# Similarities from tokens times a weight product made on the chip, in place of queries times keys

## The chip, the cores and the metric

The kernel runs on one core of a Trainium2 chip. The metric is the device time of one execution in microseconds (us). TensorE is PE in the profile (PEld are its weight loads), VectorE is DVE, ScalarE is ACT, GpSimd is POOL, and SP issues the transfers.

## The reference

x has 4 batches of 256 tokens with 256 numbers; all is float32. Four layers follow each other, each on the layer norm of x and added to x:

1. an attention whose weights come from a context of 128 numbers a token;
2. a feed-forward layer (hidden size 1024, squared ReLU) whose two weight matrices are first quantised by blocks of 64, with a search over 16 scales;
3. a gated layer in which tokens and weights are scaled by column and by row and rounded to 8-bit integers ("the quantised layer");
4. a product-key expert layer, cut to its core:

```
q = (x @ Wq).reshape(b, t, H, 2, DK)              # H = 4, DK = 64
sim1 = einsum('bthd,hkd->bthk', q[..., 0, :], keys[:, :, 0, :])   # 128 keys
sim2 = einsum('bthd,hkd->bthk', q[..., 1, :], keys[:, :, 1, :])
s1, i1 = top_k(sim1, 8); s2, i2 = top_k(sim2, 8)
final_scores, pk_idx = top_k(s1[..., None] + s2[..., None, :], 8)  # of 64 pairs
hidden = silu(x . e_down[index]) * relu(final_scores)
out = sum over heads and chosen experts of hidden * e_up[index]    # 2048 experts
```

Nothing of x stands between Wq and the keys: a similarity is x times the product of a head's Wq columns (256 by 64) and its keys (64 by 128).

## The kernel before, in words

Each engine has one queue, and its order is written out by hand as a list of calls; engines wait for each other on counting semaphores. An engine does nothing past a call whose wait is not met. Tokens go in tiles of 128: batch b has tiles t = 2b and 2b + 1. PSUM is eight banks of 128 by 512 f32.

Up to some 147 us the attention and the search over scales run (calls `unit`, `square`, `sum_error`), interleaved. Then come, on PE:

- `ffn1(i)`, 16 groups of two matmuls with 512 columns (line 626), a ReLU on ACT (line 1169), a squaring on POOL (line 347); `ffn2(b, o, tiles)`, halves of the second product of batch b (line 772), into one bank a batch. When both halves of a batch are there, `x2(b)` on DVE adds them to X (line 1861) and takes the statistics of the norm.
- the quantised layer, per batch a long chain between the engines, all its PE steps in one bank (6, or 7 for batch 1): `c_x_transposed`, `c_ratio`, `c_root`, `c_factor`, `c_diag`, `c_factors` (line 789), `c_round` (lines 1891 to 1883), `c_integers`, `c_row_scales`, `c_clip`, `c_quantised_transposed`, `c_first`, `c_h`, `c_silu`, `c_a`, then the same steps again with a 2 in their names for the second product, `c_second`, and `x3(b)` on DVE. The buffers of the layer hold two batches.
- the expert layer: `pre(b)` transposes the normed tokens into bank 6, ACT copies them (`tokens_out`). `half_queries(b, lo, hi)` multiplies them by the query weights (line 869) into banks 4 and 5, and ACT copies the queries (`queries`, line 1436). `sims(b, n)` multiplies the queries of tile t by the keys (line 882): the two sides of a key lie on rows 0 to 63 and 64 to 127 of the array and go into banks 0 and 1, four heads of 128 columns each. DVE finds the 8 largest and their places (`top8`, lines 1976 and 1982), pairs them (`pair_top8`), looks up the expert numbers (`look_up`, lines 2002 to 2018) and builds masks (`mask`, `one_hots`, lines 2038 and 2042).
- `experts(b, lo, hi)` multiplies all 2048 rows of e_down by the tokens (line 898; 8 groups a batch, into banks 4 and 5 in turn), and ACT applies the silu (`gate`, line 1454). `scatter(b, n, half)` turns masks into coefficients (line 920), ACT copies these (line 1446), POOL or, for the last tiles, DVE multiplies them by the gates (`weigh`), and `up(b, n, lo, hi)` multiplies by e_up (line 934; 16 experts' rows at a time, 16 steps a tile). `result(t)` on DVE adds the tile to X (line 2066), and SP stores it.

An f32 matmul is two records on PE in the trace. The banks make the waits: banks 0 and 1 hold the similarities of one tile until `top8` of that tile has read them; banks 4 and 5 serve queries and experts in turn, so that

```
if b:
    pe.wait_ge(s["d_g_e"], 8 * b - 1 + i)     # queries: after gates of the batch before
...
if i < 2:
    pe.wait_ge(s["d_q_e"], 2 * b + 1 + i)     # experts: after the copies of the queries
```

The functions that the diff touches, with their callers:

## Time and profile before

| what | us |
|---|---|
| median of 3 runs | 388.55 (386.41 to 388.98) |
| the profiled execution, device time | 388.38 |
| its span, first to last instruction | 386.5 |
| busy in the span: PE, DVE | 340.7, 333.8 |
| busy in the span: ACT, POOL | 246.8, 140.2 |
| mean granted TensorE clock | 0.991 |

The span is one execution, and the 1.9 us between it and its device time lie around it. A granted clock of 1 is 2.4 GHz. Matmul records overlap, so a busy sum and a piece of the chain differ by some per cent.

### The profile page before, as it was taken

What the parts mean: (1) busy time and instruction counts of PE and PEld (TensorE: products, weight loads), DVE (VectorE), ACT (ScalarE), POOL (GpSimd) and SP (SyncE); (2) the same over time, 40 slices, a digit from 0 to 9 for tenths busy, and PEclk for the clock granted to TensorE, in tenths of its full rate; (3) what the DMA queues carried; (4) which work ended last, traced back from release to release, by engine and by line L of the source; (5) the groups of instructions that cost most, each with busy time, mean ns of one, the idle gap of its engine ahead of it and who ended that gap; (6) DMA issues with size and microseconds to landing.
All of it is one profiled execution on the core that took longest, in us unless ns stands there. A gap on an engine that the chain in (4) does not pass through costs nothing.

```text
span 386.5 us, 8279 instructions
## 1 busy us (share of the span) xinstructions
PE 340.7 (88%) x3222; PEld 249.5 (65%) x3222; DVE 333.8 (86%) x838; ACT 246.8 (64%) x371; POOL 140.2 (36%) x194
## 2 busy tenths in 40 slices
PE   2898796688889889999969889998999999989997
PEld 2455453243334337688948767887888887778886
DVE  3989999999989997368877999999999999999940
ACT  3899999999998992237456687755766654011000
POOL 8737524612665644211001104255424148601000
PEclk9999999999989999999998999999999999999999
DMA  8940000000000008000000000000000000000000
GB/s 252 358 137 3 1 0 0 2 0 2 2 0 0 2 1 270 2 0 3 0 2 0 3 0 3 0 3 2 2 17 16 2 15 4 2 15 2 17 15 27
DMA packets 11142, 11.40 MB, mean 29 GB/s; under 512 B 608, under 2 KB 10592, under 8 KB 11104
## 3 DMA queue, kind: packets, MB, share of 16 engines
q1 hardware_dynamic: 11104, 10.88, 8.7%
q8 instruction: 25, 0.41, 0.5%
q14 instruction: 13, 0.11, 0.1%
HBM read 9.83 MB, written 1.05 MB: 28 GB/s over the span
## 4 chain that ended last, share of the span: by engine, by line
DVE 46%; PE 31%; ACT 11%; issue 7%; DMA 2%; POOL 1%; SPq 1%; DVEq 0%; ACTq 0%; POOLq 0%
PE pair L934 7%; DVE arena L1663 6%; PE pair L772 5%; DVE arena L1653 4%; PE pair L626 3%; DVE i L1982 3%; DVE arena L2042 3%; PE pair L898 3%; DVE s L1976 3%; ACT arena L1200 2%; ACT arena L1203 2%; DVE arena L2038 2%; DVE XN L1588 2%; DMA arena<-in_L_ffn_keys_dram 2%; PE pair L920 2%
## 5 line engine op out<-in xcount | busy, mean ns | idle before, releaser
L1663 DVE TENSOR_REDUCE arena<-arena 128x16 f32<-128x1024 f32 x64 | 66.5, 1075 | 2.5 <-POOL arena L365 1.7
L898 PE MATMUL pair<-arena,EDT 128*128 128x256 f32 x256 | 60.2, 383 | 0.0
L934 PE MATMUL pair<-EU,arena 128*128 128x256 f32 x256 | 58.4, 382 | 0.6 <-DVE arena L2066 0.6
L934 PEld LDWEIGHTS pair<-EU,arena 128*128 128x128 f32 x256 | 47.9, 190 | 7.4 <-issue 1.0
L898 PEld LDWEIGHTS pair<-arena,EDT 128*128 128x128 f32 x256 | 47.1, 190 | 6.5 <-ACT arena L1454 0.2
L644 PE MATMUL pair<-arena,WQ 128*128 128x512 fp8e4 x112 | 33.8, 383 | 15.8 <-ACT arena L1203 7.8
L488 POOL TENSOR_TENSOR arena<-arena 128x512 f32<-128x512 f32 x20 | 27.6, 1394 | 45.1 <-ACT arena L1446 45.1
L1200 ACT ACTIVATE arena<-pair,sq_bias 128x1024 f32<-128x1024 f32 x32 | 38.4, 1199 | 2.0 <-issue 1.5
L1186 ACT ACTIVATE arena<-arena,clip_bias 128x1024 fp8e4<-128x1024 f32 x32 | 39.5, 1235 | 0.0
L656 PE MATMUL pair<-arena 128*128 128x512 fp8e4 x128 | 38.6, 384 | 1.0 <-ACT arena L1186 1.0
L1454 ACT ACTIVATE arena<-pair 128x512 f32<-128x512 f32 x32 | 19.0, 598 | 27.2 <-PE pair L898 27.1
L1203 ACT ACTIVATE arena<-pair 128x1024 f32<-128x1024 f32 x32 | 35.2, 1099 | 1.2 <-PE pair L656 0.9
L365 POOL TENSOR_TENSOR arena<-arena 128x512 f32<-128x512 f32 x16 | 21.4, 1337 | 37.1 <-ACT arena L1200 37.0
L626 PE MATMUL pair<-arena 128*128 128x512 f32 x64 | 31.1, 617 | 1.3 <-ACT arena L1169 0.9
L644 PEld LDWEIGHTS pair<-arena,WQ 128*128 128x128 bf16 x112 | 8.4, 97 | 35.8 <-ACT arena L1200 13.6
L772 PEld LDWEIGHTS pair<-arena 128*128 128x128 f32 x256 | 29.5, 192 | 1.0 <-issue 1.0
L772 PE MATMUL pair<-arena 128*128 128x128 f32 x256 | 30.1, 275 | 0.0
L1653 DVE TENSOR_SCALAR arena<-arena 128x1024 fp8e4<-128x1024 f32 x32 | 28.5, 893 | 1.7 <-PE pair L656 1.7
L347 POOL TENSOR_TENSOR arena<-arena 128x512 f32<-128x512 f32 x16 | 17.3, 1090 | 29.4 <-ACT arena L1169 24.8
L1446 ACT COPY arena<-pair 128x512 f32<-128x512 f32 x20 | 19.6, 1073 | 9.9 <-PE pair L920 9.9
L920 PEld LDWEIGHTS pair<-arena 64*128 64x128 bf16 x1536 | 20.2, 93 | 6.2 <-issue 3.2
L920 PE MATMUL pair<-arena 64*128 64x32 bf16 x1536 | 21.6, 173 | 1.9 <-DVE arena L2060 1.2
(201 smaller groups left out, 666.1 us busy)
## 6 DMA issues: line engine op xcount, KB each, us to landing
arena<-in_L_ffn_e_down_dram SPq DMA_DIRECT2D x1, 2048.0 KB, 12.5
EU<-in_L_ffn_e_up_dram SPq DMA_DIRECT2D x1, 2048.0 KB, 9.2
arena<-in_L_ffn_w_fc_dram SPq DMA_DIRECT2D x2, 512.0 KB, 5.4
X<-in_x_dram SPq DMA_DIRECT2D x1, 1024.0 KB, 6.2
arena<-in_L_ffn_w_proj_dram SPq DMA_DIRECT2D x1, 1024.0 KB, 13.7
GUW<-in_fside_BxS2xS_dram SPq DMA_DIRECT2D x1, 1024.0 KB, 11.4
out_dram<-arena SPq DMA_DIRECT2D x8, 128.0 KB, 1.7
CTX<-in_ctx_dram SPq DMA_DIRECT2D x1, 512.0 KB, 4.9
```

The lines of the kernel that those rows point to most:

```text
L626: last = pe.matmul(bank[2 + i % 2], W1T[:, k, m * P:m * P + P], xnT[:, k, half * 512:half * 512 + 512], start=(k == 0), stop=(k == 1))
L644: pe.matmul(to[half], stepN[:, j - 2, :], qr[:, (g - 2) % QDEEP, cols[half]], start=False, stop=False, skip_group_check=True)
L656: last = pe.matmul(to[half], stepI[:, j, :], qr[:, g % QDEEP, cols[half]], start=False, stop=True, skip_group_check=kept)
L772: last = pe.matmul(bk2(F2_BANK[b])[:, n, o * P:o * P + P], h2T[:, k, at:at + P], W2T[:, k, o * P:o * P + P], start=(k == 0), stop=(k == HI ...
L898: last = pe.matmul(bk2(4 + i % 2)[:, r, :], EDT[:, k, at:at + P], xT4[:, b % 2, k, :], start=(k == 0), stop=(k == 1))
L920: last = pe.matmul(bank[scatter_bank(t, half) + r][:, g16 * JW:g16 * JW + JW], oh[rows, g // NG, :, g % NG], wc[rows, c, g // NG, :, g % N ...
L934: last = pe.matmul(bk2(7)[:, n, :], PR[:, n, e, :], EU[:, e, :], start=(e == 0), stop=(e == EROWS - 1))
L1186: act.activation(qr[:, g % QDEEP, :], qu[:, g // NS % 2, :], ACT.Relu, bias=clip_bias[:, 0:1], scale=-GRID / STEPS[g % NS], saturate=False ...
L1200: act.activation(qd(g), pair[2 + g % 2][:, :], ACT.Square, bias=sq_bias[:, g % NS:g % NS + 1]).then_inc(s["squared"], 1)
L1203: act.activation(qd(g), pair[2 + g % 2][:, :], ACT.Square).then_inc(s["squared"], 1)
L1653: dve.tensor_scalar(qr[:, g % QDEEP, :], qu[:, g // NS % 2, :], TB_MAX * STEPS[g % NS], GRID / STEPS[g % NS], ALU.min, ALU.mult, saturate= ...
L1663: dve.tensor_reduce(err[:, g // NS % 2, :, g % NS], squares, AX.X, ALU.add).then_inc(s["reduced"], 1)
```

## The change

Queries are no longer formed. Once, PE transposes the query weights (`query_weights_transposed`, 8 transposes, copied by ACT to WQT) and multiplies them by the keys (`key_weights`, two calls of 8 matmuls with 64 rows, copied by ACT to WK). WK is a matrix of 256 by 1024: model dimension by side, head and key. `sims` then multiplies the tokens of a tile by WK: per side two matmuls with 128 rows and 512 columns. `half_queries` and `queries` go. All queues of the part after the search are put in a new order (PE, ACT, DVE; on POOL the calls of `weigh`, `ranks` and `coefficient_parts`). In it the ffn2 halves of batch 1 stand before ffn1(9), batches 0 and 1 pass through the quantised layer side by side, `pre(0)` gets a wait for `c_ratio` of batch 2 and `pre(2)` waits for `c_pre` of batch 3 where it waited for its `c_ratio`; each of these steps uses the same bank.

```diff
-        qT4 = cut(22 * KI, 2 * KI).rearrange("p (s h t) -> p s h t", s=2, h=H)
+        WK = cut(22 * KI, 2 * KI).rearrange("p (k a n) -> p k a n", k=2, a=2)
+        WQT = cut(24 * KI, KI).rearrange("p (h d) -> p h d", h=H)
...
-            def half_queries(b, lo, hi_):
...
+            def query_weights_transposed():
+                pe.wait_ge(ld["wq1"], 16)
+                pe.wait_ge(s["wT_e"], 8)
+                pe.wait_ge(s["guwT_e"], B)
+                for h in range(H):
+                    for k in range(2):
+                        last = pe.transpose(bk2(h // 2)[:, h % 2, k * P:k * P + P], WQ1[:, k, h * P:h * P + P],
+                                            ident[:, :])
+                last.then_inc(s["wqT_t"], 1)
+            def key_weights(k):
+                pe.wait_ge(s["wqT_e"], 2)
+                if k:
+                    pe.wait_ge(s["wk_e"], 2 * k)
+                for h in range(H):
+                    for a in range(2):
+                        rows = slice(a * DK, a * DK + DK)
+                        last = pe.matmul(bank[a][:, h * NK:h * NK + NK], WQT[rows, h, k * P:k * P + P],
+                                         keysT[rows, h, :], start=True, stop=True)
+                last.then_inc(s["wk_t"], 1)
             def sims(b, n):
                 t = 2 * b + n
                 if not t:
-                    pe.wait_ge(s["guwT_e"], B)
-                pe.wait_ge(s["d_q_e"], 2 * b + 2)
+                    pe.wait_ge(s["wk_e"], 4)
+                pe.wait_ge(s["d_xT_e"], b + 1)
                 if t:
                     pe.wait_ge(s["d_simread"], t)
-                for h in range(H):
-                    for a in range(2):
-                        last = pe.matmul(bank[a][:, h * NK:h * NK + NK],
-                                         qT4[a * DK:a * DK + DK, b % 2, h, n * P:n * P + P],
-                                         keysT[a * DK:a * DK + DK, h, :], start=True, stop=True)
+                for a in range(2):
+                    for k in range(2):
+                        last = pe.matmul(bank[a], xT4[:, b % 2, k, n * P:n * P + P], WK[:, k, a, :],
+                                         start=(k == 0), stop=(k == 1))
...
             def experts(b, lo, hi_):
-                    if i < 2:
-                        pe.wait_ge(s["d_q_e"], 2 * b + 1 + i)
+                    if i == 0:
+                        pe.wait_ge(s["d_xT_e"], b + 1)
+                    if g < 2:
+                        pe.wait_ge(s["x2"], g + 1)
                     else:
                         pe.wait_ge(s["d_g_e"], g - 1)
...
             ffn1(8)
             pe.wait_ge(s["squared"], NU)
             pe.wait_ge(s["hsq"], 8)
             ffn2(0, 0)
+            ffn2(1, 0)
             w_transposed(NCH - 1)
             gate_weights_transposed(0)
+            gate_weights_transposed(1)
             pe.wait_ge(s["wT_e"], 8)
             ffn2(0, 1).then_inc(s["f2_t"], 1)
+            ffn2(1, 1).then_inc(s["f2_t"], 1)
+            c_x_transposed(0)
+            ffn1(9)
+            ffn1(10)
+            c_x_transposed(1)
...
+            query_weights_transposed()
+            c_factors2(0)
+            c_factors2(1)
             ffn2(3, 0)
+            key_weights(0)
...
+            pe.wait_ge(s["c_ratio"], 3)
             pre(0)
+            c_second(1)
+            key_weights(1)
+            experts(0, 0, 1)
             pe.wait_ge(s["d_xT_e"], 1)
+            c_factors(2)
+            experts(0, 1, 2)
             sims(0, 0)
+            experts(0, 2, 3)
             pe.wait_ge(s["c_pre"], 3)
             pre(1)
+            experts(0, 3, 4)
+            sims(0, 1)
...
+            c_factors(3)
+            up(0, 0, 12, 16)
+            pe.wait_ge(s["c_pre"], 4)
             pre(2)
+            up(0, 1, 0, 12)
...
+            up(1, 1, 0, 16)
             pre(3)
+            up(2, 0, 0, 4)
             sims(3, 0)
```

## Rows read from the trace of the kernel before

**Rows 1.** the page, busy time of each engine (share of the span) and its instructions
```profile
PE 340.7 (88%) x3222; PEld 249.5 (65%) x3222; DVE 333.8 (86%) x838; ACT 246.8 (64%) x371; POOL 140.2 (36%) x194
```

**Rows 2.** the page, busy tenths in 40 equal slices of the span (9.66 us each)
```profile
PE   2898796688889889999969889998999999989997
...
DVE  3989999999989997368877999999999999999940
```

**Rows 3.** windows: length, busy time of each engine, granted TensorE clock, DMA share, GB/s
```profile
155.00:180.00 25.00, 24.17 (x164) 18.88 (x163) 14.73 (x37) 10.03 (x21) 5.20 (x5) 1.00 0.01 2
180.00:195.00 15.00, 14.59 (x131) 14.40 (x130) 12.20 (x39) 8.44 (x20) 0.00 (x0) 1.00 0.00 1
195.00:212.00 17.00, 13.69 (x88) 11.11 (x88) 12.57 (x46) 10.75 (x22) 1.93 (x2) 0.90 0.00 1
...
235.00:343.10 108.10, 103.79 (x1468) 88.75 (x1468) 104.17 (x362) 61.77 (x99) 48.95 (x56) 1.00 0.02 7
343.10:383.90 40.80, 40.11 (x632) 34.82 (x632) 28.09 (x65) 1.79 (x3) 1.43 (x6) 1.00 0.04 12
144.17:383.90 239.73, 226.69 (x2744) 191.76 (x2744) 201.81 (x630) 113.14 (x200) 64.37 (x80) 0.99 0.05 16
```

**Rows 4.** the chain that ended last, pieces on PE: start, length, line, records
```profile
174.16 1.72 PE pair L626 x4
...
176.32 0.44 PE pair L526 x4
...
183.43 1.79 PE pair L772 x16
...
203.79 5.06 PE pair L869 x16
...
211.03 1.09 PE pair L882 x16
...
344.50 3.65 PE pair L898 x16
...
351.61 5.18 PE pair L934 x24
...
376.70 7.16 PE pair L934 x32
```

**Rows 5.** groups of PE's instructions from 144 us on: busy, mean ns, idle before
```profile
L869 PE MATMUL pair<-arena,WQ 128*128 128x256 f32 x64 | 16.7, 413 | 0.0
...
L882 PE MATMUL pair<-keysT,arena 64*128 64x128 f32 x128 | 9.2, 284 | 0.8 <-DVE i L1982 0.8
```

**Rows 6.** windows, the stretch of the first queries, columns as in rows 3
```profile
203.00:206.00 3.00, 3.00 (x11) 2.50 (x11) 2.64 (x13) 1.49 (x3) 0.00 (x0) 0.58 0.00 0
```

**Rows 7.** timeline, DVE's two first sums of f2 onto X
```profile
159.77 0.69 DVE L1861 TENSOR_TENSOR X<-X,pair 128x512 f32<-128x512 f32 x1 [7.12 <-PE pair L772]
...
174.27 0.69 DVE L1861 TENSOR_TENSOR X<-X,pair 128x512 f32<-128x512 f32 x1 [0.58 <-PE pair L772]
```

**Rows 8.** waits of PE, 144 to 235 us: total, times, longest
```profile
PE pair L836 <- ACT arena L1426: 1.9, 2, 1.3
```

**Rows 9.** the chain that ended last, pieces on DVE
```profile
264.41 1.67 DVE s L1976 x8
266.10 2.23 DVE i L1982 x9
...
271.06 0.18 DVE rin L1883
271.31 0.10 DVE pab L2003
...
273.92 0.36 DVE ctxT L2018
...
326.37 1.68 DVE s L1976 x8
```

**Rows 10.** groups of ACT's instructions from 235 us on
```profile
L1436 ACT COPY arena<-pair 128x512 f32<-128x512 f32 x6 | 3.4, 575 | 2.1 <-PE pair L869 2.1
```

409 lines of the change are left out of this document (184 added, 225 removed).

## The prediction

> **What bounds the kernel now.** I read the page first, for the shares of busy time: PE 88%, DVE 86%, ACT 64% [rows 1]. A mean over such different stages says little, so next the forty slices [rows 2]: DVE has a hole in slices 16 to 22 (145 to 212 us), deepest in the 17th, and PE is nearly full to the end. Then the windows by stage [rows 3]. The change touches only what follows the last search unit of the weight quantiser, so the ledger runs from 144.17 us, where the last ffn1 groups run, to 383.9, where the last up-projection matmul ends. In these 239.73 us PE is busy for 226.69 and idle for 13.0. From 235.0 to 343.1 PE is busy 103.8 of 108.1 us and DVE 104.2 of 108.1: both are full. In the last 40.8 us PE is busy 40.1, and DVE only 28.1. The chain of waits says the same in another form: it runs on DVE up to 343 us [rows 9], then on PE to the end [rows 4]. So the end is set by PE's total work plus its idle time, and DVE decides how much idle time PE gets. ACT has room (61.8 of 108.1) and counts only where PE or DVE stands behind one of its copies.
>
> **PE's work: what goes.** The queries of a batch are 16 matmul records. Their busy sum for four batches is 16.7 us [rows 5]. As a piece of the chain one batch takes 5.06 us [rows 4], and that one ran partly at a granted clock of 0.58, 1.2 GHz for most of the stretch [rows 6], in a stretch of 17 us (195 to 212) in which PE was idle for 3.3 [rows 3]. At full clock a record of 256 columns takes 0.228 us (3.65 us for 16, experts, [rows 4]), so 3.65 us a batch. The old similarities of a tile are 16 records of 128 columns on 64 rows each, and take 1.09 us [rows 4]; eight tiles are 8.7 us by that, 9.2 by busy time [rows 5].
>
> **PE's work: what comes.** New similarities are, for each tile, 2 sides by 2 halves of the model dimension: 4 matmuls with 128 rows and 512 columns in f32, 8 records. The trace has that form in ffn1: 4 records in 1.72 us [rows 4], so 0.43 us a record and 3.44 us a tile. Eight tiles: 27.5 us. The change trades 64-row matmuls, which run two at a time, and a short query step for twice the multiplications, since a key row that had 64 numbers has 256 now. Besides, once: 8 transposes of the query weights at 0.11 us (4 take 0.44, [rows 4]), 0.9 us; and the product with the keys, twice 16 records of exactly the old similarities' form, 2.2 to 2.3 us.
>
> The sum by pieces of the chain: added 27.5 + 0.9 + 2.2 = 30.6, removed 8.7 + 5.06 + 3 x 3.65 = 24.7, net +5.9 us. By busy sums: 30.7 less 25.9, net +4.8. I take +5.4. Nothing hides this, for PE is the engine that is full. With no idle time at all the span would be some 7.6 us shorter than now (5.4 - 13.0); that is the floor.
>
> Why the old similarities are so cheap bears on the sum. Their records of 128 columns cost 0.068 us each on 64 rows, while a 128-row record of 128 columns costs 0.112 (ffn2, 16 in 1.79 us, [rows 4]): the two halves of the array overlap, though not fully. The Trainium skill speaks against this change at this point ("TensorE: Matmul & The Clock Gate", Why this matters for your kernels): a matmul with a short contraction takes as long as a full one, and the gain is that tiles run concurrently. With perfect pairing a tile would have cost 0.89 us and not 1.09, and the net would be some 1.6 us larger than by the row; the measured row decides.
>
> **ACT and the banks.** ACT loses 8 copies of queries at 0.58 us and gains 2 + 4 of the same size [rows 10]; a gain of about 1 us on an engine with room: nothing. What the missing query step frees is a wait: experts of a batch no longer stand behind the copies of queries out of banks 4 and 5, nor the queries behind the last gates of the batch before. PE hardly waits there now; its longest named wait is for a copy of the quantised layer, 1.9 us in two times [rows 8]. I price it within the idle time below.
>
> **The new order, first part (144 to about 215 us).** I walked the three queues with the durations of the trace. The second batch's f2 sum starts on DVE at 174.27 now [rows 7]. In the new order both halves of batches 0 and 1 are done before ffn1(9), and that sum can start at 162.9; the first stays at 159 (159.77 now). From there batches 0 and 1 pass through the quantised layer side by side, one serving as the other's cover. PE's work from 144.2 up to the end of sims(0, 0), by the prices above with all the small matmuls of the layer, is 66.8 us; the walk ends it at 215.9, so with 4.9 us of idle time: 2.0 between 179 and 184 (the integers' transposes stand behind ACT's copies), 1.2 around 200 (second rounding of batch 0), 0.7 around 206 (pre(0) now waits for the ratio of batch 2), the rest in crumbs. Now sims(0, 0) ends at 212.1 (211.03 + 1.09, [rows 4]) with 4.55 us idle (0.83 + 0.41 + 3.31, [rows 3]) and 1.4 us lost to the clock (5.06 - 3.65). By 215.9 the new order has done 3.9 us of work that is still open now at 212.1.
>
> **Second part.** Each tile's top8 takes 4 us on DVE (1.67 for the maxima, 2.23 for the indices, [rows 9]) and blocks the two banks for the next tile's similarities. After sims(0, 0) PE has experts, pre(1) and experts, 1.8 + 0.44 + 1.8 us, while top8(0) takes 4.05: covered to the tenth. Most of the rest of the walk looks like this, with DVE now waiting for PE (1 to 2 us at seven places, as a tile's similarities arrive 2.35 us later after the order to start) rather than PE for DVE. Where PE does stand: about 2 us before pre(2), which now waits until DVE has read the factors of batch 3 (a look-up of 3.0 and a rounding of 2.9 us are ahead, [rows 9]); 0.65 before pre(3) and 0.6 before up(2, 0) (a result is queued on DVE behind x3(3)); 1.3 in the last three up-projections, behind results and one_hots(7). That is some 5.3 us after 215.9, with crumbs, where PE now has 8.5 from 212 on (13.0 - 4.55). The walk ends the last matmul at 386.9 instead of 383.9.
>
> **How the numbers follow.** The walk's idle time is 4.9 + 5.3 = 10.2 us against 13.0 now. A walk with fixed durations is too smooth: it has none of the stretched instructions of DVE beside POOL, and each step that comes late in these in-order queues stops PE for what it is late. I therefore take 12 us of idle time, nearer to the 13.0 of the trace than to zero. The profiled execution took 388.38 us for a span of 386.5; the median of the runs is 388.55, 0.17 more, which I leave aside. 388.38 + 5.4 - 1.0 = 392.8 us. No change that is under 1%, some 3.9 us, can be told from none here, so my forecast lies just above that line.
>
> **Rivals.**
> A. The walk is right as it stands: idle time 10 us or a little less, 390 to 391.5 us, which is "no change". For it: batches 0 and 1 run in tandem and DVE's hole is filled (14.7 of 25 us busy from 155 to 180, [rows 3]). Together with the part of my forecast's spread that falls under the line: 0.43.
> B. Forecast, slower by over 1%: work +5.4, idle time 11.5 to 15: 0.36.
> C. Starvation: DVE becomes the bound of the first part. Between 159 and 215 us the walk has DVE without a pause of more than 1 us, and both batches meet on it at once; if each of its some 60 short steps costs 0.05 to 0.1 us more, x3(0) and with it pre(0), the tokens and sims(0, 0) come 3 to 6 us later, PE has only experts that need the same tokens, and stands. From 17 us of idle time on it gives 397 to 400. If PE is idle enough there for the clock to fall to 1.2 GHz again, as it did after 200 us [rows 6], 1.4 us or so come on top. Against it: it is DVE's work that moved into its own hole. 0.12.
> D. The other side: the order is worth more than the work costs. It needs less than 4 us of idle time from 144 us on for 384 us, against 13.0 now. The mechanism would be the removed step between tokens and similarities: queries and their copies are 3.65 + 0.58 us of latency for each batch now, the similarities become 2.35 longer, so DVE gets its top8 some 1.9 us earlier for the same tokens, never pauses, and PE always has a scatter or an up-projection ready. Against it: at 343 us the chain leaves DVE, and what PE does then it does back to back, so DVE's advance is no shortening; the floor is 380.8. Or a 512-column record is cheaper than in ffn1, which two rows of the same form exclude. 0.09.
>
> The range holds 8 times in 10 if it leaves out most of D and the far end of C: 386 to 398.5 us (idle time from 5 to 18). Slower by over 1%: B and C, 0.48. Within 1%: 0.43. Faster: 0.09.
>
> **What the profile after would show.** Similarities of a tile: 8 records in 3.44 us, 64 in all, busy 27 to 28 us. PE busy from ffn1(8) to the last up-projection some 232 us. x2 of batch 1 at about 163 us and top8(0) at about 216. PE's idle time after 144 us near 12. Top8(6) starts at about 333 us where it is at 326.4 now [rows 9]. The last 40 us still PE without gaps. I am wrong if the records of the similarities take less than 0.4 us, if PE's idle time is under 8 us (the order worth more than I saw) or over 17 (C), or if the walk's first part ends far from 216 us.

## The result, and the profile after

The changed kernel takes 400.42 us (median of 4 runs, 399.65 to 400.49); the kernel before took 387.48 on the same chip (4 runs, 385.66 to 388.98). The ratio is 1.0342, with a 95% interval of 1.0298 to 1.0385: slower by some 13 us, where 392.8 was forecast with a range to 398.5. The profiled execution took 400.47 us for a span of 398.6, which is 12.1 more than the 386.5 of before.

The page of the changed kernel, busy times and three of its rows of slices (now 9.97 us each), against [rows 1] and [rows 2]:

```profile
PE 348.3 (87%) x3134; PEld 244.8 (61%) x3134; DVE 337.4 (85%) x838; ACT 240.5 (60%) x365; POOL 141.0 (35%) x194
...
PE   2898786688788989988989999986999996999997
...
DVE  3989999999999993795889897899699899679870
...
PEclk9999999999999999999999999998999998999999
```

DVE's hole of slices 16 to 22 is filled in part: from 155 to 180 us DVE is busy for 19.5 of 25 us where it was for 14.7 [rows 3], but it still pauses for 1.6, 2.0 and 1.1 us between 181 and 191.3 us. PE has two new holes, in slices 28 and 34, each with a dent of the granted clock in the same slice. The windows of the changed kernel, columns as in [rows 3]:

```profile
144.17:396.00 251.83, 234.54 (x2652) 187.25 (x2652) 204.22 (x628) 106.59 (x193) 62.51 (x79) 0.99 0.05 15
144.17:216.23 72.06, 66.05 (x477) 53.95 (x478) 54.65 (x149) 36.66 (x83) 10.44 (x11) 1.00 0.10 34
235.00:343.10 108.10, 98.64 (x1325) 76.69 (x1324) 93.75 (x280) 56.24 (x87) 45.46 (x44) 0.97 0.02 7
343.10:396.00 52.90, 51.54 (x766) 42.65 (x764) 39.23 (x113) 4.78 (x8) 2.86 (x12) 1.00 0.03 9
270.00:280.00 10.00, 6.96 (x27) 5.67 (x26) 9.72 (x42) 4.38 (x9) 1.75 (x2) 0.83 0.04 15
330.00:340.00 10.00, 6.32 (x21) 4.30 (x20) 9.00 (x14) 1.87 (x2) 0.89 (x1) 0.83 0.04 15
```

The first row is the ledger of the prediction, from 144.17 us to the end of the last up-projection: 251.83 us against 239.73, which is all of the 12.1. PE is busy for 234.54 us of it (226.69 before) and idle for 17.3 (13.0 before). By chance the search ended 1.96 us earlier in this execution (139.34 against 141.30), so that at 144.17 it had 1.95 us more of PE's work behind it; the table of all runs, below, counts from that end. The last two rows are the new holes, and in both DVE is busy for 9 us or more of ten: PE waits there for an engine that is at work. The last 53 us are nearly full, as they were (1.4 us idle; 0.7 of 40.8 before).

Pieces of the chain of waits of the changed kernel (start, length, line, records), against [rows 4] and [rows 9]. L878 is the product of query weights and keys, L891 the new similarities, L944 the up-projection, L1982 the maxima of `top8`:

```profile
206.79 1.09 PE pair L878 x16
...
212.78 3.45 PE pair L891 x8
...
216.25 1.70 DVE s L1982 x8
...
275.52 6.48 PE pair L944 x24
...
335.48 3.20 PE pair L944 x8
...
338.68 3.89 PE pair L891 x8
...
342.57 1.73 PE pair L944 x8
```

24 records of the up-projection take 5.18 us at full clock [rows 4] and 6.48 here, right behind the first hole; 8 records take 1.73 and, behind the second, 3.20; similarities take 3.45 and, behind that, 3.89. So the lower clock takes 1.30 + 1.47 + 0.44 = 3.2 us behind the two holes. Groups of PE's instructions from 144 us on:

```profile
L944 PE MATMUL pair<-EU,arena 128*128 128x256 f32 x256 | 61.2, 394 | 2.2 <-DVE arena L2072 2.0 <-issue 0.2
...
L891 PE MATMUL pair<-arena 128*128 128x512 f32 x64 | 29.4, 603 | 0.2 <-DVE i L1988 0.2
...
L878 PE MATMUL pair<-keysT,arena 64*128 64x128 f32 x32 | 2.3, 285 | 0.0
```

Waits of PE in the changed kernel from 144 us to the end (total, times, longest):

```profile
PE pair L525 <- DVE XN L1594: 4.3, 2, 3.3
PE pair L525 <- DVE rin L1889: 3.0, 1, 3.0
...
PE pair L788 <- ACT arena L1368: 1.7, 1, 1.7
```

L525 is the transposes of `pre`. Of the first row, 3.3 us are the wait ahead of pre(3), for DVE's normed tokens (L1594); the second row, 3.0 us, is the wait ahead of pre(2), until DVE has read the factors of batch 3 (L1889). The wait of L788, 1.7 us, is ahead of `c_factors(3)`, which stands before pre(2) in PE's queue.

### The profile page after: what moved, and what is told of

Same layout as the page of the kernel before. It is cut to its first block, busy times and chain, and to the rows that moved or that the text cites. A ratio compares the mean times of both kernels' runs of the same rounds, so it can differ in the third digit from the quotient of the medians.

```text
span 398.6 us, 8095 instructions
## 1 busy us (share of the span) xinstructions
PE 348.3 (87%) x3134; PEld 244.8 (61%) x3134; DVE 337.4 (85%) x838; ACT 240.5 (60%) x365; POOL 141.0 (35%) x194
## 4 chain that ended last, share of the span: by engine, by line
PE 45%; DVE 31%; ACT 14%; issue 6%; DMA 2%; POOL 1%; SPq 1%; ACTq 0%; DVEq 0%; POOLq 0%
PE pair L908 11%; PE pair L944 9%; PE pair L891 7%; PE pair L771 5%; DVE arena L1669 5%; PE pair L930 4%; ACT arena L1204 3%; ACT arena L1207 3%; ACT arena L1190 3%; DVE arena L1659 2%; DMA arena<-in_L_ffn_keys_dram 2%; DVE i L1988 2%; PE pair L525 2%; DVE s L1982 1%; DVE stats L1581 1%
## 5 line engine op out<-in xcount | busy, mean ns | idle before, releaser
L944 PE MATMUL pair<-EU,arena 128*128 128x256 f32 x256 | 61.2, 394 | 2.2 <-DVE arena L2072 2.0
L908 PE MATMUL pair<-arena,EDT 128*128 128x256 f32 x256 | 59.2, 382 | 0.0
L944 PEld LDWEIGHTS pair<-EU,arena 128*128 128x128 f32 x256 | 49.4, 197 | 10.7 <-issue 3.0
L643 PE MATMUL pair<-arena,WQ 128*128 128x512 fp8e4 x112 | 33.6, 381 | 15.1 <-ACT arena L1207 7.8
L489 POOL TENSOR_TENSOR arena<-arena 128x512 f32<-128x512 f32 x20 | 29.3, 1477 | 30.6 <-ACT arena L1457 30.6
L366 POOL TENSOR_TENSOR arena<-arena 128x512 f32<-128x512 f32 x16 | 21.7, 1353 | 35.4 <-ACT arena L1204 35.3
L625 PE MATMUL pair<-arena 128*128 128x512 f32 x64 | 30.1, 598 | 1.3 <-ACT arena L1173 0.9
L891 PE MATMUL pair<-arena 128*128 128x512 f32 x64 | 29.4, 603 | 0.2 <-DVE i L1988 0.2
L466 POOL CAST i12f<-i 128x64 bf16<-128x64 uint32 x8 | 7.1, 888 | 62.1 <-DVE i L1988 44.2
L348 POOL TENSOR_TENSOR arena<-arena 128x512 f32<-128x512 f32 x16 | 17.1, 1074 | 33.8 <-ACT arena L1173 29.2
L1659 DVE TENSOR_SCALAR arena<-arena 128x1024 fp8e4<-128x1024 f32 x32 | 27.3, 854 | 0.6 <-PE pair L655 0.6
```

The lines of the kernel that those rows point to most:

```text
L625: last = pe.matmul(bank[2 + i % 2], W1T[:, k, m * P:m * P + P], xnT[:, k, half * 512:half * 512 + 512], start=(k == 0), stop=(k == 1))
L643: pe.matmul(to[half], stepN[:, j - 2, :], qr[:, (g - 2) % QDEEP, cols[half]], start=False, stop=False, skip_group_check=True)
L891: last = pe.matmul(bank[a], xT4[:, b % 2, k, n * P:n * P + P], WK[:, k, a, :], start=(k == 0), stop=(k == 1))
L908: last = pe.matmul(bk2(4 + i % 2)[:, r, :], EDT[:, k, at:at + P], xT4[:, b % 2, k, :], start=(k == 0), stop=(k == 1))
L944: last = pe.matmul(bk2(7)[:, n, :], PR[:, n, e, :], EU[:, e, :], start=(e == 0), stop=(e == EROWS - 1))
L1659: dve.tensor_scalar(qr[:, g % QDEEP, :], qu[:, g // NS % 2, :], TB_MAX * STEPS[g % NS], GRID / STEPS[g % NS], ALU.min, ALU.mult, saturate= ...
```

## What the executions add up to

The search ends between 139.2 and 141.7 us, differently from one execution to the next. So the table counts from the end of the last matmul group of the search to the start of the last result on DVE, and gives PE's and DVE's busy time in that stretch of the profiled execution. "Clock" is my estimate of the part of PE's busy time that a granted clock under 1 cost: over windows of 5 us, the sum of busy time times (1 - granted clock). It gives 3.2 us for the changed kernel, as the records above do, and 1.5 for the kernel before, where the records of the first queries say 1.4 (5.06 - 3.65, [rows 4]). A stretch is one execution: the profiled one of e8 is 4.2 us above its median, that of e10 and e5 2 above. Times are in us; each ratio is against the kernel before on the same chip, and where two kernels of different chips are compared, the ratios are the better guide (0.01 is 3.9 us).

| kernel | median | ratio (95%) | stretch | PE busy | of it clock | PE idle | DVE busy |
|---|---|---|---|---|---|---|---|
| before | 387.48 | 1 | 242.6 | 228.7 | 1.5 | 13.9 | 204.4 |
| after | 400.42 | 1.0342 (1.0298 to 1.0385) | 256.6 | 238.5 | 3.2 | 18.2 | 208.7 |
| e1_pre2 | 399.58 | 1.0348 (1.0274 to 1.0423) | 256.0 | 238.3 | 2.6 | 17.8 | 211.4 |
| e2_pre3 | 396.17 | 1.0266 (1.0197 to 1.0336) | 252.9 | 238.0 | 2.8 | 14.9 | 208.0 |
| e3_both | 394.88 | 1.0248 (1.0185 to 1.0311) | 250.7 | 235.6 | 0.0 | 15.1 | 210.6 |
| e4_algorithm_alone | 401.66 | 1.0391 (1.0315 to 1.0467) | 257.3 | 240.2 | 6.7 | 17.1 | 203.8 |
| e5_order_alone | 404.18 | 1.0415 (1.035 to 1.0481) | 262.2 | 235.9 | 6.7 | 26.2 | 207.5 |
| e6_half_product | 391.08 | 1.0072 (1.0031 to 1.0113) | 245.6 | 225.9 | 3.9 | 19.7 | 207.7 |
| e7_half_one_hot | 398.67 | 1.0307 (1.0239 to 1.0375) | 254.5 | 237.7 | 2.9 | 16.8 | 199.9 |
| e8_batch3_early | 403.62 | 1.0415 (1.0358 to 1.0471) | 262.0 | 241.5 | 5.8 | 20.5 | 209.2 |
| e9_filled_holes | 403.62 | 1.0433 (1.0386 to 1.0481) | 258.1 | 243.0 | 3.0 | 15.1 | 208.6 |
| e10_short_weigh | 390.60 | 1.0093 (1.0067 to 1.0119) | 246.6 | 235.7 | 1.3 | 10.9 | 198.5 |
| e11_short_weigh_before | 382.36 | 0.9882 (0.9824 to 0.994) | 237.3 | 227.7 | 1.5 | 9.6 | 197.2 |
| e12_filled_before | 387.58 | 1.0009 (0.9979 to 1.0039) | 243.5 | 230.1 | 1.5 | 13.5 | 205.3 |
| e13_weigh_twice_after | 409.80 | 1.0595 (1.0544 to 1.0646) | 265.4 | 240.5 | 5.5 | 24.9 | 215.8 |
| e14_weigh_twice_before | 398.78 | 1.0285 (1.0222 to 1.0348) | 254.1 | 233.6 | 5.5 | 20.5 | 214.3 |
| e15_both_short_weigh | 389.95 | 1.01 (1.0069 to 1.0132) | 245.5 | 234.7 | 0.0 | 10.7 | 198.8 |
| e16_algorithm_short_weigh | 399.37 | 1.0336 (1.0281 to 1.0391) | 254.7 | 239.1 | 5.3 | 15.6 | 198.2 |

## First question: do the two holes cost what they show?

The two holes and the clock behind them show 3.0 + 1.7 + 3.3 + 3.2 = 11.2 us, where the walk had some 2.7 us of idle time and no clock: more than the 7.6 us to the forecast. The first theory was that they are faults of the written order and that closing them gives their time back. The rival was that PE stands there because DVE is late with everything, so that a hole closed in one place opens in another.

**e1_pre2**: pre(2) goes ahead of the column factors of batch 3, and the first experts of batch 2 right behind these; ACT's copy of the tokens moves ahead too.

```diff
-            c_factors(3)
-            up(0, 0, 12, 16)
-            pe.wait_ge(s["c_pre"], 4)
+            pe.wait_ge(s["c_ratio"], 4)
             pre(2)
...
+            up(0, 0, 12, 16)
...
+            c_factors(3)
+            experts(2, 0, 2)
             up(0, 1, 0, 12)
```

> The kernel after, with the step pre(2) ahead of the factors of batch 3 again, two groups of experts of batch 2 right behind them, and ACT's copy of these tokens ahead of the diagonals of batch 3. Theory H (two holes): of the 12.1 us by which PE ends later, this place has 3.0 us of idle time before pre(2), 1.7 before the factors and 1.2 us lost to the clock that fell behind it (24 records in 6.48 us instead of 5.3). It should give back 4 to 5 us: 395 to 397 us, with no stretch under full clock near 275 us. Theory W (work): PE's and DVE's queues only move the idle time elsewhere, since the end is set by work and by DVE's total; less than 1.5 us comes back, 399 us or more.

The ratio did not move: 1.0348 against 1.0342, so the 4 to 5 us that the first theory asked for did not come. Windows of e1, then the same three of the changed kernel, columns as in [rows 3]:

```profile
260.00:280.00 20.00, 18.06 (x179) 15.17 (x178) 19.34 (x69) 10.75 (x20) 6.88 (x10) 1.00 0.03 9
280.00:300.00 20.00, 18.77 (x268) 14.62 (x268) 18.56 (x64) 11.91 (x17) 7.77 (x11) 1.00 0.01 3
300.00:320.00 20.00, 18.07 (x351) 14.30 (x350) 19.61 (x39) 10.65 (x18) 11.28 (x10) 1.00 0.03 9
```

```profile
260.00:280.00 20.00, 15.27 (x159) 12.73 (x158) 19.31 (x73) 10.63 (x20) 7.21 (x10) 0.91 0.03 9
280.00:300.00 20.00, 20.00 (x276) 15.80 (x275) 16.43 (x60) 10.08 (x14) 7.96 (x9) 1.00 0.01 2
300.00:320.00 20.00, 19.59 (x359) 15.72 (x357) 17.91 (x34) 11.78 (x20) 14.21 (x10) 1.00 0.03 9
```

In the first window PE does 2.8 us more and keeps its clock. In the next two it loses 1.2 and 1.5 us that it had not lost before, and the wait ahead of pre(3) is still 3.3 us. The idle time moved. The rival held here, as far as one edit shows it: what PE lacked was not work in its queue but what DVE had yet to make.

**e2_pre3**: on DVE the normed tokens and the result of batch 3's turn go ahead of a look-up and a mask; on PE the similarities go ahead of the up-projection.

```diff
             x3(3)
-            look_up(5)
             ln_apply(3, 2, "ln4")
-            mask(5)
+            look_up(5)
             result(3)
+            mask(5)
...
             pre(3)
-            up(2, 0, 0, 4)
             sims(3, 0)
-            up(2, 0, 4, 8)
+            up(2, 0, 0, 8)
```

> The kernel after, with the norm of batch 3 ahead of the look-up of tile 5 on DVE, result(3) before its mask, and sims(3, 0) ahead of the first steps of up(2, 0) on PE. Theory H: PE stands 3.3 us before pre(3), 0.4 before up(2, 0), and loses 1.4 + 0.45 us to the clock behind it (8 records in 3.20 us instead of 1.78, 8 in 3.89 instead of 3.44): 4 to 5.5 us come back, 395 to 396.5 us. Theory W: the look-up that is put off comes late for the scatter of tile 5, and less than 1.5 us comes back.

4.3 us by the medians, 2.9 by the ratios (1.0266). The intervals of the two ratios overlap, but the slowest of e2's four runs (398.81) is below the fastest of the changed kernel's (399.65). The wait of pre(3) fell from 3.3 to 1.0 us and PE's idle time by 3.3. This edit changes the order of DVE, the late engine, and that of PE as well; no run has DVE's part alone.

**e3_both**: both edits.

```diff
+            pe.wait_ge(s["c_ratio"], 4)
+            pre(2)
...
+            experts(2, 0, 2)
...
             x3(3)
+            ln_apply(3, 2, "ln4")
             look_up(5)
-            ln_apply(3, 2, "ln4")
+            result(3)
```

> Both edits together. Theory H: the gains add to 8 to 10 us, 390.5 to 392.5 us, near what my walk gave before the result. Theory W: under 3 us, 397.5 or more.

5.5 us by the medians, 3.6 by the ratios (1.0248), 5.9 by the stretch of the profiled executions, where neither theory had put it (8 to 10, or under 3). Of the 5.9, 3.1 are idle time and 2.8 busy time: the granted clock is 1.00 in all of this execution's stretch. It is the best version of the changed kernel that computes the reference, and still some 2.5% above the kernel before.

**e8_batch3_early**: e3, and the second half of batch 3's quantised layer moved forward on all queues.

```diff
+            scatter(1, 0, 1)
+            experts(2, 4, 5)
...
+            c_factors2(3)
+            experts(2, 5, 7)
             up(0, 1, 12, 16)
```

> The kernel with both edits of the third run, and the second half of the quantised layer of batch 3 moved forward on all three queues (its x3 ahead of one_hots(4), about 9 us earlier). Theory O: x3(3) at 316 us instead of 326 brings tokens and sims(3, 0) forward, 388 to 391 us. Theory S: PE is the one that is late, work only changes places, 392.5 to 396 us.

Slower than e3 by 1.7% of the time before, and outside what either theory allowed. The profiled execution is 4.2 us above the median, so its parts say only where the loss can lie: idle time 20.5 instead of 15.1 us, and 5.8 us for the clock where e3 lost none. Its first `top8` comes 79.3 us after the end of the search, where e3's comes after 76.9, so 2.4 us are lost before the edit begins, with a fall of the clock that is told at the end; a second fall stands at 330 us. That batch 3's layer was merely placed too late is not what the run shows.

## Second question: the algorithm or the order?

**e4_algorithm_alone**: the kernel before with similarities from the product, queries and their copies taken out, its order otherwise kept.

```diff
+            query_weights_transposed()
...
+            key_weights(0)
...
-            half_queries(0, 0, 2)
...
-            half_queries(1, 0, 1)
```

> The kernel before in its old order, with the queries taken out and the weight product put in (its steps where the idle time around batch 0 lies), the new similarities in the places of the old. Theory H: the algorithm costs its work on PE, +5.4 less what the missing query step frees: 391 to 395 us, and no hole of 3 us. Theory W says the same or more, up to 398, since the old order was fitted to short similarities. A third one, O (order): the new algorithm is worth something in itself and the new order alone is to blame; then this is at 388 us or less.

1.0391, above every theory's figure. PE's longest waits in it, columns as in [rows 8]; L827 is the factors for the second product of the quantised layer, which wait for ACT's diagonals, and L932 turns masks into coefficients. Then a window behind the longest of them, columns as in [rows 3]:

```profile
PE pair L827 <- ACT arena L1379: 5.1, 2, 2.9
PE pair L932 <- DVE arena L2052: 4.0, 1, 4.0
```

```profile
330.00:335.00 5.00, 5.00 (x91) 2.80 (x84) 4.72 (x8) 2.33 (x3) 4.77 (x7) 0.52 0.01 3
```

The three waits, of 2.9, 2.1 and 4.0 us, each stand ahead of a stretch at a low clock: 0.51 from 205 to 210 us, 0.66 from 245 to 250, 0.52 from 330 to 335. By the table the stretch is 14.7 us longer than before: 3.2 of it idle time, 5.2 the clock, and 6.3 the rest of PE's busy time. So most of what the old order loses on the new algorithm beyond its work is the clock behind a few long waits.

**e5_order_alone**: the changed kernel's order with queries and similarities as before.

```diff
-            query_weights_transposed()
...
-            key_weights(0)
...
-            key_weights(1)
...
+            half_queries(0, 0, 2)
+            c_factors(2)
             experts(0, 0, 1)
...
-                        last = pe.matmul(bank[a], xT4[:, b % 2, k, n * P:n * P + P], WK[:, k, a, :],
+                                         qT4[a * DK:a * DK + DK, b % 2, h, n * P:n * P + P],
+                                         keysT[a * DK:a * DK + DK, h, :], start=True, stop=True)
```

> The new order of the kernel after with the old algorithm: queries formed, 64-row similarities; each batch's queries stand right before the first thing that needs them (before the factors of batch 2, the first experts of batch 1, up(0, 1), and up(2, 0)). PE has some 6 us less work than the kernel after. Theory S (similarities, formed after the first four runs: the algorithm costs on every tile both PE's time and a later top8, whatever the order): at least 6 us under the kernel after, 388 to 394 us, and each top8 with less wait for PE. Theory O (the new order is bad by itself, through batch 3's late x3): 396 us or more, since DVE's order is unchanged and x3(3) stays behind one_hots(4).

1.0415, the highest ratio of the four (its interval overlaps that of the next), although PE has less work than in the changed kernel: its idle time is 26.2 us, and the clock costs 6.7. The theory that the new order is bad by itself had asked for 396 us or more. The queries had to be given places in an order made without them, each right before its first use, and other places were not tried. With this the square is: both old 387, new algorithm alone +3.9%, new order alone +4.2%, both +3.4%. Neither half can be called the cause by itself. It looks as if each order fits its own algorithm, and the new order hardly repays the new algorithm its cost (1.0342 against 1.0391, inside the intervals).

## Third question: is it PE's work or DVE's?

**e6_half_product**: only the first 128 of the 256 numbers of a token are multiplied, 4 records a tile.

```diff
-                    for k in range(2):
-                        last = pe.matmul(bank[a], xT4[:, b % 2, k, n * P:n * P + P], WK[:, k, a, :],
-                                         start=(k == 0), stop=(k == 1))
+                    last = pe.matmul(bank[a], xT4[:, b % 2, 0, n * P:n * P + P], WK[:, 0, a, :],
+                                     start=True, stop=True)
```

> The kernel after with half of each similarity: only the first 128 of the 256 numbers of a token are multiplied, so 4 records a tile and 1.72 us instead of 3.44, 13.8 us less on PE, everything else the same. Theory S: 9 to 14 us come back, 387 to 391 us, since DVE waits for PE before the tiles and PE for DVE behind them. A DVE-bound theory, D: DVE is full from 261 to 335 us, so under 6 us come back, 394.5 us or more.

The edit takes away 8 x 1.72 = 13.8 us of PE's time and gives back 9.3 by the medians, 10.4 by the ratios (1.0072). So two thirds to three quarters of the work that was taken away come back; the rest shows as idle time (19.7 us in the profiled execution) and 3.9 us of clock. Of the ten runs, the two with a mean granted clock of 0.996 took 386.9 us, and there nearly the whole 13.8 came back; the eight at 0.982 took 388.2 to 391.5. So part of what is missing goes with the clock.

**e7_half_one_hot**: DVE builds its one-hot masks for half of the slots; the other half is zero.

```diff
-                dve.tensor_tensor(oh, iotaI.unsqueeze(1).to_broadcast([P, NO, P, NG]), over(t, 1, P), ALU.is_equal)
+                dve.tensor_tensor(oh[:, 0:NO // 2], iotaI.unsqueeze(1).to_broadcast([P, NO // 2, P, NG]),
+                                  over(t, 1, P)[:, 0:NO // 2], ALU.is_equal)
```

> The kernel after with half of the one-hot matrix: DVE builds it for 32 of 64 slots only, the other half stays zero, 1.1 us less on DVE for each of 8 tiles (one of 2.2 us becomes 1.1), 8.8 in all, PE the same. Theory D: 5 us or more come back, 395 us or less. If PE's work sets the end, under 2.5 us, 398 us or more.

DVE has 8.8 us less to do, and the time falls by 1.75 us (medians; 1.4 by the ratios, inside the intervals). DVE's sum is not what counts. It fits that the masks lie where DVE has room, and that what counts is DVE's time on the stretch from `x3` to the normed tokens; this run does not show the second half.

## Fourth question: what makes DVE late ahead of pre(2) and pre(3)?

The timeline of the changed kernel there: start, us, engine, line, operation. First DVE, then POOL's `weigh` (L489) of the same stretches:

```profile
260.95 1.18 DVE L1993 TENSOR_TENSOR arena<-s 128x256 f32<-128x256 f32 x1
...
264.44 1.17 DVE L1876 TENSOR_SCALAR tmpa<-m_xs 128x2 f32<-128x2 f32 x1
...
267.40 1.75 DVE L2013 TENSOR_TENSOR arena<-iota,pab 128x512 bf16<-128x512 f32 x1
...
313.35 2.28 DVE L2044 TENSOR_TENSOR arena<-arena,ctxT 128x4096 bf16<-128x4096 bf16 x1
315.55 2.84 DVE L2048 TENSOR_TENSOR arena<-arena,ctxT 128x3072 bf16<-128x3072 bf16 x1
...
328.43 1.26 DVE L2009 TENSOR_SCALAR pab<-pk 128x32 uint32<-128x32 uint32 x1
329.73 1.71 DVE L2013 TENSOR_TENSOR arena<-iota,pab 128x512 bf16<-128x512 f32 x1
```

```profile
260.57 1.28 POOL L489 TENSOR_TENSOR arena<-arena 128x512 f32<-128x512 f32 x1 [1.15 <-ACT arena L1457]
...
264.31 1.28 POOL L489 TENSOR_TENSOR arena<-arena 128x512 f32<-128x512 f32 x1
...
267.33 1.27 POOL L489 TENSOR_TENSOR arena<-arena 128x512 f32<-128x512 f32 x1 [1.74 <-ACT arena L1457]
...
313.39 3.37 POOL L489 TENSOR_TENSOR arena<-arena 128x512 f32<-128x512 f32 x1 [1.04 <-ACT arena L1457]
...
328.34 2.54 POOL L489 TENSOR_TENSOR arena<-arena 128x512 f32<-128x512 f32 x2
```

The second row is a step on 128 by 2 numbers, and it takes 1.17 us. POOL's multiplication beside it began 0.13 us earlier and ends at 265.59; DVE's step ends at 265.61. The third row ends at 269.15, 0.55 us after POOL's end at 268.60. At 328.43 a step on 32 numbers takes 1.26 us; the first of POOL's two multiplications ends about then (328.34 + 1.27 = 329.61). It goes the other way too: POOL's 3.37 us from 313.39 on begin just behind DVE's L2044, which ends at 315.63; 1.27 later would be 316.9, and POOL ends at 316.76. DVE's L2048, which began at 315.55, takes 2.84 us, where such a step takes 1.75 to 1.81 in e10. So whoever comes second seems to stand still until the other is done, and DVE's loss is up to the length of one of POOL's multiplications each time. Not every step is held: of DVE's instructions that started beside a multiplication of POOL, those that find maxima and their places, the reductions, and the sums that read PSUM took their usual time, while steps with two inputs in SBUF and most with a scalar (TENSOR_SCALAR) did not. A reduction beside POOL's multiplication of 269.53 to 270.80, then the step behind it, which takes 0.24 us in e10:

```profile
269.64 0.69 DVE L2017 TENSOR_REDUCE isel<-arena 128x64 f32<-128x512 bf16 x1
270.36 0.48 DVE L2020 TENSOR_SCALAR pack<-isel,slot 128x32 bf16<-128x32 f32 x1
```

The Trainium skill says it in these terms ("SBUF — State Buffer", SBUF: two separate sides): VectorE and GpSimd share one pair of ports; an instruction of VectorE needs it in a two-port mode, or with two inputs in SBUF beside a GpSimd instruction that reads SBUF; whichever starts first holds it for the whole instruction, and the other blocks. The trace agrees: the three DVE steps of 0.17, 0.43 and 0.73 us (e10, below) end 0.02, 0.28 and 0.55 us after POOL's multiplication, so each ends 0.15 to 0.18 us sooner than if its own whole time had followed POOL's end.

**e10_short_weigh**: POOL multiplies 1 of the 16 expert rows of each group, so its 1.27 us become 0.25; the other rows stay unmultiplied.

```diff
-                    w = pv[:, :, 2 * r:2 * r + 2, 16 * half:16 * half + 16]
-                    pool.tensor_tensor(w, w, gv[:, :, 2 * r:2 * r + 2, 16 * half:16 * half + 16], ALU.mult
+                    w = pv[:, 0:1, 2 * r:2 * r + 2, 16 * half:16 * half + 16]
+                    pool.tensor_tensor(w, w, gv[:, 0:1, 2 * r:2 * r + 2, 16 * half:16 * half + 16], ALU.mult
```

> The kernel after with POOL's multiplications of coefficients by gates cut to one of 16 expert rows for tiles 0 to 4 (the other rows stay unmultiplied), so that DVE's steps are not stretched beside POOL. In the trace after, steps of DVE next to POOL take 1.71 us instead of 0.70 (comparison of the look-up), 1.26 instead of 0.10, 2.84 instead of 1.67. Theory P (ports): that is what made DVE 6 us late at x3(3), and 4 us or more come back, 396 us or less. Theory S: it is in the kernel before as well, so under 2 us here.

390.6 us: 9.8 less than the changed kernel (9.6 by the ratios), with not one instruction of DVE or PE changed. The same steps of DVE in e10, and PE's two waits:

```profile
263.83 0.43 DVE L1993 TENSOR_TENSOR arena<-s 128x256 f32<-128x256 f32 x1
...
266.58 0.17 DVE L1876 TENSOR_SCALAR tmpa<-m_xs 128x2 f32<-128x2 f32 x1
...
268.54 0.73 DVE L2013 TENSOR_TENSOR arena<-iota,pab 128x512 bf16<-128x512 f32 x1
```

```profile
PE pair L525 <- DVE rin L1889: 1.8, 1, 1.8
...
PE pair L525 <- DVE XN L1594: 1.3, 2, 1.0
```

From the first step of x3(2) (L1968) to the next `top8` DVE needs 16.6 us in the changed kernel (258.07 to 274.65) and 13.3 in e10 (261.24 to 274.54), for the same instructions. 1.00 + 1.02 + 0.75 of these 3.3 us are the three rows; the rest are two other steps beside POOL, of 0.98 and 0.48 us, which take 0.69 and 0.24 in e10. DVE's busy time falls by 10.1 us and PE's idle time by 7.3, to 10.9; the clock costs 1.9 less, since neither fall behind the two holes is left. A rival would be that POOL's results come sooner. But in both kernels no instruction waits for POOL's 20 multiplications, by the profile, so their lateness was not what PE or DVE stood for.

**e11_short_weigh_before**: the same edit in the kernel before.

```diff
-                    w = pv[:, :, 2 * r:2 * r + 2, 16 * half:16 * half + 16]
+                    w = pv[:, 0:1, 2 * r:2 * r + 2, 16 * half:16 * half + 16]
```

> The same cut in the kernel before, as the control. Theory P says less than half of what the kernel after gains; theory S that both gain the same, 0 to 3 us.

0.9882, some 4.2 us (4.6 by the ratio), for 7.2 us less of DVE's busy time. So, all that hangs on them included, the stretched steps beside `weigh` cost the kernel before about 4.5 us and the changed kernel 9.7, and without most of them the distance between the two kernels is 390.6 - 382.4 = 8.2 us. By the profiled executions it is 9.3, of which 8.0 are PE's busy time and 1.3 idle time.

**e13_weigh_twice_after** and **e14_weigh_twice_before**: a second multiplication on POOL, of the same size and read by nobody, behind each of the 20, in either kernel.

```diff
+                    link(pool.tensor_tensor(scr, EU[:, 0:2, :], EU[:, 2:4, :], ALU.mult))
```

> The kernel after with a second multiplication of the same size on POOL behind each of the 20 of weigh, with a result that nobody reads (20 x 1.1 to 1.4 us, POOL is idle for far longer than that). Theory P (port): DVE's steps beside POOL are stretched twice as often, DVE's busy time rises by 5 to 10 us, and the time by 3 to 8 us. Theory L (latency of the weighted coefficients): the real results come at most 1.4 us later in a row, DVE is as before, and the time rises by less than 2 us.

> The same second multiplications in the kernel before. Theory P: DVE's busy time rises here too, the time by half as much as after or less, 1 to 4 us. Theory L: under 2 us for both.

+9.4 us (9.8 by the ratios) in the changed kernel and +11 to 12 in the kernel before. DVE's busy time rises by 7.1 and 9.9 us though it has nothing more to do. PE's waits in e13, at the very places of the two holes:

```profile
PE pair L528 <- DVE XN L1597: 6.7, 2, 5.8
PE pair L528 <- DVE rin L1892: 5.8, 1, 5.8
```

3.3 became 5.8 and 3.0 became 5.8: the holes are where DVE's stretched time shows. The other half of the expectation fell: the kernel before was to bear the added load with less loss than the changed one, and it bore it no better. Of the 11.6 us by which its stretch grew, 6.6 are idle time and some 4 the clock (1.5 us in the kernel before, 5.5 here). One of its new waits is an idle stretch of 3.0 us that the profile puts down to "issue", so what it waited for there stays open.

**e15_both_short_weigh**: the edits of e3 and of e10 together. **e16_algorithm_short_weigh**: those of e4 and of e10.

```diff
-                    w = pv[:, :, 2 * r:2 * r + 2, 16 * half:16 * half + 16]
+                    w = pv[:, 0:1, 2 * r:2 * r + 2, 16 * half:16 * half + 16]
```

> The two edits of the third run with the short multiplications. If the two holes are where the stretched DVE time shows (one loss seen twice), the gains don't add: 388 to 390.5 us, 0 to 2.5 under the short multiplications alone. If they are two losses, they add: 384 to 386 us.

> The new algorithm in the old order with the short multiplications. If the old order suffers from the longer similarities by itself, it gains like the kernel before, about 4 us, and stays near 397 us; if port and tight places act together as in the kernel after, it gains 8 us or more, 393 us or less.

e15: 1.01, where e10 alone has 1.0093. e3's gain of 4 to 5 us is gone once DVE is hardly held up: both remove the same loss. e16: 1.0336, only some 2 us below e4, and its wait of PE for ACT is still 4.9 us in two times (5.1 in e4). So in the old order the new algorithm loses its time without POOL, to its work and to the clock behind long waits; why those waits are long (I take it that the longer similarities stand ahead of the quantised layer's steps) is not shown. In the new order some 5 of the 13 us (9.7 - 4.5) are DVE beside POOL.

## Fifth question: does the clock cost what it shows?

**e9_filled_holes**: five matmuls whose result nobody reads ahead of pre(2), six ahead of pre(3), each group begun as soon as its bank is free. **e12_filled_before**: three ahead of pre(0) in the kernel before, where [rows 6] show the clock at 0.58.

```diff
+            def filler(n, at):
+                for i in range(n):
+                    pe.matmul(bk2(at)[:, i % 2, :], EDT[:, 0, 0:P], EU[:, 0, :], start=True, stop=True)
...
+            filler(5, 4)
...
+            filler(6, 4)
```

> The kernel after with idle matmuls (results not used, into a free bank) put into its two holes: 5 matmuls of 256 columns before the wait of pre(2), 6 before pre(3), 2.2 and 2.7 us for holes of 3.0 and 3.3. If the clock falls because PE stands there, it stays at full speed and the records behind run at 0.22 and 0.43 us again: 1.2 + 1.9 = some 3 us less, 396.5 to 398 us, idle time in the count 4.9 less and busy time 2 more. If the two lost stretches of clock cost nothing, because DVE is what is late behind them, 399.5 to 401 us.

> The kernel before with 3 idle matmuls (1.3 us) before pre(0), where PE stands 1.4 us and the clock falls for the queries of batch 0 (16 records in 5.06 us instead of 3.65). If they keep the clock up, 1 to 1.4 us less than before, 0.3%; if the fall comes from the earlier gaps at 195 to 198 us as well, no difference, or 0.3 us more.

Windows of e9, then two of e12, columns as in [rows 3]:

```profile
180.00:190.00 10.00, 7.62 (x48) 6.57 (x48) 5.57 (x12) 7.40 (x11) 1.04 (x1) 0.66 0.01 3
270.00:280.00 10.00, 7.42 (x39) 6.05 (x38) 9.55 (x29) 3.79 (x8) 2.54 (x2) 1.00 0.00 0
330.00:340.00 10.00, 8.92 (x43) 7.40 (x42) 9.69 (x20) 2.16 (x3) 3.34 (x6) 1.00 0.04 13
```

```profile
203.00:206.00 3.00, 3.00 (x17) 2.70 (x16) 2.83 (x12) 1.85 (x5) 1.46 (x2) 1.00 0.00 0
340.00:350.00 10.00, 9.79 (x128) 8.45 (x129) 9.86 (x41) 1.20 (x2) 1.43 (x6) 0.83 0.01 2
```

The clock did what was asked of it at the three places: 1.00 behind them, where it was 0.83, 0.83 and 0.58. But in both executions it fell somewhere else. In e12 the window from 340 us on is at 0.83, and 16 records of experts (L898) there take 5.34 us where the same ones take 3.65 in the kernel before [rows 4]; the wait ahead of them is 1.2 us in both. Up to that place e12 was 1.1 us ahead of the kernel before, counted from the end of the search (200.75 against 201.83 us), so the first queries at full clock had given most of their 1.4 us; the new fall took 1.7 back. Its 1.4 us more of PE's busy time are then the three added matmuls (6 records, 1.4 us at [rows 4]'s 0.228), with the clock costing 1.5 us in either kernel. The medians say the same for the whole: 1.0009, with an interval of 0.3% to either side. e9 is slower than the changed kernel (1.0433, against 1.0342), and outside both of its expectations; its fall at 180 to 190 us costs 3.0 us, about what the two old ones did, and its added matmuls (22 records, 5.0 us by the same figure) fill only 3.1 us of idle time. So whether the 3.2 us behind the two holes would come back is not shown; a run without the early fall would have been needed.

## Why the prediction was wrong

Forecast were +5.4 us of work and -1.0 of idle time; the ledger says +7.85 of busy time and +4.3 of idle time. Of the 7.85, 3.2 are the clock behind the two holes, and 1.95 belong on top, since the search ended earlier. So PE's work without the clock rose by 4.7 us by the ledger and by 6.6 counted from the end of the search.

- **PE's work: right in kind, some 1 us too small.** Similarities take 3.43 to 3.49 us a tile in the chain (3.44 forecast) in six of the eight tiles, 3.69 in one and 3.89 in the one behind the second hole; there are 64 records, and the key product takes 1.09 us for each half. The net is 6.6 against 5.4. Most of the difference is one term: by busy time the similarities are 29.4 us, where "27 to 28" was forecast and 27.5 stood in the sum of busy times, priced from pieces of the chain beside old ones priced by busy time. PE's 234.5 us against the "some 232" hold the 3.2 us of clock and lack the 1.95 of the early start. A record costs 0.43 us, so the reason stands as well: 64-row matmuls that run in pairs were traded for twice the multiplications. e6 gave back two thirds to three quarters of the work it took away, by the median, and with POOL nearly out of the way (e10 against e11) PE's busy time is 8.0 of the 9.3 us between the kernels.
- **The first part: nearly right.** Batch 1's sum of f2 began at 160.94 us (162.9 forecast, and 21.6 us after the end of the search in both). sims(0, 0) ended at 216.23 (215.9). From 144.17 on PE was busy for 66.05 us and idle for 6.0, where I had 66.8 and 4.9. Counted from the end of the search it came 2.3 us late, half of it work and half idle time. DVE's hole was filled in part, and PE was not starved. The walk had DVE without a pause of more than 1 us between 159 and 215 us; the trace has three, of 1.6, 2.0 and 1.1 us.
- **The step that failed is "I therefore take 12 us of idle time".** It was 17.3, and 11.3 of it in the second part, where the walk had 5.3. The walk itself, with fixed durations, gave 10.2 us and 390 to 391.5 us in all; e10, in which POOL hardly holds DVE up, has 10.9 us idle and took 390.6. So the walk described a kernel without stretched steps, and what I put on top for them, 1.8 us, was nearness to the 13.0 of the kernel before and no price from a row. Shortening the multiplications behind them gives 9.8 us. Nor was the walk compared with its like: its 10.2 us, without stretched steps, stood against 13.0 with them, and looked like a gain. On equal terms the idle time rises, from 9.6 to 10.9 us with short multiplications (e11, e10) and from 13.9 to 18.2 with whole ones. That e10 lands on the walk's total is therefore luck in part: its own control, e11, is at 382.4. What was to be "about 2 us before pre(2)" was 1.7 + 3.0, and the "0.65 before pre(3)" 3.3. The trace of the kernel before had such steps: two groups of its DVE instructions from 235 us on are these (line, form, count, busy us and mean ns):

```profile
L2016 DVE TENSOR_TENSOR pack<-isel,hi 128x32 bf16<-128x32 f32 x7 | 2.3, 329 | 0.2
...
L1871 DVE TENSOR_SCALAR tmpb<-m_ws 128x2 f32<-128x2 f32 x1 | 1.3, 1251 | 0.0
```

The second began at 261.57 us, beside two multiplications of POOL that ran from 260.26 to 262.79; the other three of its kind took 0.16 us. A step on 128 by 2 numbers with 1.25 us should have been priced: the steps on the chain to pre(2) and pre(3) that can be held, at up to one of POOL's multiplications more, three or four times, for 3 to 4 us a hole by my estimate (1.27 us each, less what is left of it when they start).
- **The clock was not in the sum.** I had priced its fall once, in rival C, and in the wrong place. It shows 3.2 us behind the two holes, against the 1.4 behind the first queries that went with them.
- **How much is POOL.** The kernels are 12.9 us apart by the medians, where the forecast had 4.4, and still 8.2 us apart with short multiplications in both. So DVE beside POOL is somewhat over half of the 8.5 us that were missed; the rest is in PE's work, the clock, and idle time that the new order has anyway.
- **Top8(6)** was forecast at 333 us and started at 342.6. The idle time ahead of pre(2) and pre(3) above what the walk gave these places is 2.7 + 2.7 us, the clock behind them 3.2, and the first part ended 0.3 later: 8.9 of the 9.6.
- **Rivals.** A, "the walk is right", is refuted for the kernel as it stands; e10 has its idle time and its total, with the reserve just told. C gave the size, 17 us idle and 397 to 400 us, and had the wrong place and cause: the first part did not starve, and it was not many short steps being each a little longer, but a few being longer by what was left of a multiplication of POOL. D, that the order is worth more than the work, is refuted by the result itself, and e5 shows that the new order gave the old algorithm nothing.

What stays open: why the new order costs the old algorithm so much idle time (e5) and whether its queries stood in the best places, what makes e4's waits long, what the "issue" gap in e14 is, and which part of the clock's loss would come back if it did not fall. A version of the changed kernel in which POOL's multiplications are issued clear of DVE's chain wasn't tried. None of the versions that compute the reference beats the kernel before.

## What to carry to other kernels

Before merging two products into one, count the columns and the form of the matmuls: here a chain of short contractions that ran two at a time cost less than the single product. When a new order is walked through with the durations of a trace, give every DVE step that can fall beside a POOL operation, and is of a kind that was held in a trace, a second price, and look for those steps on the chain ahead of each wait of the full engine. Compare a walk with a walk of the kernel before, not with its trace. Leave room for the clock behind the long waits: here 1.3 and 1.9 us behind the two holes. And when a hole is to be closed, look first at the engine that is late: the edit that left DVE's queue alone (e1) moved the idle time, and the one with DVE's queue in it (e2) gave time back, though DVE's part was not tried by itself.

## What the hardware showed that was not expected

- A DVE step of 128 by 2 numbers took 1.17 us beside POOL and 0.17 without; one of 128 by 512, 1.75 and 0.73. The loss, 1.0 us in both, goes with what is left of POOL's instruction and not with the step's own size. A reduction of 128 by 512 numbers took 0.69 us beside POOL and 0.69 without.
- 20 multiplications of 1.27 us on an engine that is busy for a third of the span cost the changed kernel 9.8 us, two fifths of their 25.4, though nobody waited for their results.
- The clock does not fall each time after the same idle time. Up to 190 us these kernels have the same instructions, and from 180 to 190 us they had: e6 2.65 us idle and 1.00; e8 and e9 2.4 and 0.66; e10 2.4 and 0.83; the changed kernel 1.1 and 1.00; e2 0.8 and 0.83.
- In the profiled executions of e3 and e15 the clock did not fall at all in the stretch; in those of e4 and e5 it cost 6.7 us by the table, and in e4 it fell behind three waits of 9.1 us in all.
- Matmuls that nobody reads kept the clock up at the three places where they stood, in one profiled execution each; it fell at another place in both, and no time was gained.
